# Row transposes placed between two projections, reordered queues and identity products in a fused attention and expert kernel

## The reference

```python
q = einsum('bse,hed->bhsd', x, Wq) + bq      # 16 heads of 64; k and v alike
scores = where(causal, q @ k.T / sqrt(64), -inf)
out = softmax(scores) @ v                    # heads joined: 1024 columns
x = layernorm(x + out @ Wo + bo)
xn = layernorm(x) * gamma + beta
probs = softmax((xn @ router_w.T) / 1.5)
w, idx = top_k(probs, 2)                     # 8 experts, 2 for each token
y = sum over the two experts of w * (silu(xn @ W1[e]) @ W2[e])
x = layernorm(y + x)
```

## Time and profile before

| | |
|---|---|
| Time, median of 3 runs | 1347.1 us (1345.36 to 1347.86) |
| Time of the profiled execution | 1345.8 us |
| Its span | 1344.0 us |
| PE busy | 1297.7 us, 97% |
| DVE busy | 1116.6 us, 83% |
| ACT busy | 1037.2 us, 77% |
| POOL busy | 491.7 us, 37% |
| Chain that ended last | PE 93%, ACT 2%, DVE 2% |

### The profile page before, as it was taken

How to read it: one execution, slowest core, us unless ns; L and a number is a source line. 1 busy time by engine, 2 the same in 40 slices (tenths; PEclk the granted TensorE clock), 3 DMA queues, 4 the chain that set the end, 5 groups by cost and what they waited for, 6 DMA issues and landing times.

```text
span 1344.0 us, 35085 instructions
## 1 busy us (share of the span) xinstructions
PE 1297.7 (97%) x10918; PEld 1134.5 (84%) x10918; DVE 1116.6 (83%) x5412; ACT 1037.2 (77%) x3402; POOL 491.7 (37%) x1067
## 2 busy tenths in 40 slices
PE   6999999999999999999999999999998999999967
PEld 5888888888888888888888888888887999999953
DVE  6888888888888888888888888888886898888847
ACT  7888888888888888888888888888884555555527
POOL 1023333333333333333333333333335665555545
PEclk9999999999999999999999999999999999999989
DMA  2000000000000000000000000000033777666638
GB/s 82 2 5 17 16 16 19 13 14 13 14 13 13 14 14 14 13 14 18 16 18 15 14 13 14 13 14 14 14 140 114 216 221 219 213 214 209 205 123 327
DMA packets 67641, 89.74 MB, mean 67 GB/s; under 512 B 10352, under 2 KB 37107, under 8 KB 67456
## 3 DMA queue, kind: packets, MB, share of 16 engines
q1 hardware_dynamic: 57808, 70.28, 16.6%
q0 software_dynamic: 8640, 17.13, 3.8%
q10 hardware_dynamic: 1008, 0.08, 0.1%
HBM read 61.66 MB, written 26.71 MB: 66 GB/s over the span
## 4 chain that ended last, share of the span: by engine, by line
PE 93%; ACT 2%; DVE 2%; issue 1%; DMA 1%; POOL 0%; ACTq 0%; POOLq 0%; SPq 0%; DVEq 0%
PE ps_f L1036 15%; PE ps_b L1070 14%; PE ps_a L1036 13%; PE ps_s L1077 12%; PE ps_s L1058 10%; PE ps_s L1235 9%; PE ps_b L1244 5%; PE ps_a L1244 5%; PE ps_s L1061 4%; PE ps_s L1311 2%; PE ps_a L1226 1%; ACT probs L574 1%; PE ps_f L1102 1%; PE ps_s L1082 1%; ACT probs L576 1%
## 5 line engine op out<-in xcount | busy, mean ns | idle before, releaser
L574 ACT ACTIVATE probs<-probs,neg_max 128x256 f32<-128x256 f32 x512 | 255.3, 499 | 127.8 <-DVE neg_max L790 125.4
L786 DVE CUSTOM_DVE_ANT_0 probs<-ps_s,mask 128x256 f32<-128x256 f32 x512 | 214.4, 419 | 37.1 <-PE ps_s L1061 34.3
L450 POOL TENSOR_SCALAR ln_b<-mv 128x2 f32<-128x2 f32 x32 | 6.1, 190 | 637.4 <-DVE mv L853 637.4
L1070 PE MATMUL ps_b<-pt,f_y 128*64 128x256 f32 (+1 forms) x2048 | 196.0, 333 | 10.3 <-ACT f_y L569 7.3
L660 ACT ACTIVATE m_tanh<-ps_s 128x256 f32<-128x256 f32 x284 | 108.8, 384 | 124.7 <-PE ps_s L1235 114.8
L1077 PE MATMUL ps_s<-ident,probs 128*128 128x128 f32 x1536 | 204.7, 274 | 0.0
L576 ACT ACTIVATE probs<-probs,neg_max 128x128 f32<-128x128 f32 x512 | 198.7, 388 | 0.0
L800 DVE TENSOR_SCALAR probs<-probs,inv_sums 128x256 f32<-128x256 f32 x512 | 180.8, 353 | 9.1
L1070 PEld LDWEIGHTS ps_b<-pt,f_y 128*64 128x64 f32 x2048 | 132.0, 137 | 61.0 <-issue 16.3
L540 POOL DMA_INDIRECT y_tok<-m_y,m_dest x142 | 139.7, 984 | 111.5 <-DVE m_dest L946 79.4
L1058 PE MATMUL ps_s<-qk 64*128 64x256 f32 x1024 | 171.3, 408 | 7.9 <-ACT pt L605 1.7
(11 more groups left out here) (193 smaller groups left out, 2988.5 us busy)
## 6 DMA issues: line engine op xcount, KB each, us to landing
m_w<-in_w SPq DMA_DIRECT2D x142, 256.0 KB
m_x<-queue SPq DMA_DIRECT2D x71, 133.0 KB, 3.0
f_y<-y_tok SPq DMA_DIRECT2D x32, 256.0 KB, 6.5
queue<-empty SPq DMA_DIRECT2D x8, 532.0 KB, 5.0
x_raw<-in_x SPq DMA_DIRECT2D x32, 128.0 KB, 2.1
out_x<-f_y SPq DMA_DIRECT2D x16, 256.0 KB, 5.7
y_tok<-m_y,m_dest POOLq DMA_INDIRECT x142
queue<-z,slot_now POOLq DMA_INDIRECT x128, 2.4
```

Source lines behind the costliest of these rows:

```text
L574: act.activation(row[:, 0:2 * P], row[:, 0:2 * P], ACT.Exp, scale=-1.0, bias=neg_max[:, pair, h, 0:1], accum_out=sums[:, d % 2, pair, h, 0:1])
L786: dve.tensor_tensor_reduce(out=row[:, 0:2 * P], in0=ps_s[:, pair, h, 0:2 * P], in1=mask[:].rearrange("p a b -> p (a b)"), scale=-1.0, scal ...
L1070: ins = pe.matmul(ps_b[r, cols], v[:, k, c * P + h * DH:c * P + (h + 1) * DH], pt[:, pair, h, src], start=(k == 0), stop=(k == 1), skip_gr ...
```

## The change

Seven edits:

1. *Rows between the projections.* In step q == 3 TensorE transposes `z` between the q and k projections of pair 0 and pair 1, into the banks of pair 1, behind waits for `z_done` and for the last maxima; it waits for `xnt_done` ahead of the transposes of pair 1. ScalarE does the `xnt` scaling ahead of both `evacuate_qk` and `first_pt`. The scores of pair 0 no longer wait for `xnt_done`.
2. *Start.* ScalarE rounds the second half of the weights behind the first two `evacuate_qk`. VectorE makes their rests in step 0 (two) and step 1 (one).
3. *Table.* Parts 3 to 6 do what 4 to 7 did, one step earlier.
4. *Step 127.* VectorE does `second_pt` ahead of `normalise(d, 1)`.
5. *Last expert steps.* `rows(68)` moves from j = 70 to j = 69, behind `rows(67)`; `rows(69)` goes ahead of `keep(70)`.
6. *Ranks.* `ranks(SEQS)` goes behind `output(0)` at j = 1.
7. *Identity products.* TensorE multiplies `ident` by `ident`, six times behind the first transposes and 42 times behind `output(NJ - 1)`. Nothing reads the results.

```diff
@@ -579 @@ scalar
-            for half in range(2):
+            def round_weights(half, i):
                 cols = slice(half * 512, (half + 1) * 512)
...
+            for i in range(3):
+                round_weights(0, i)
             act.wait_ge(small_loaded, 16 * 7)
             act.wait_ge(biases_ready, 1)
             evacuate_qk(0, 0)
             evacuate_qk(0, 1)
+            for i in range(3):
+                round_weights(1, i)
@@ -620 @@ scalar, step
+                if q == 3 and n in MID:
+                    act.wait_ge(zt_ready, n)
+                    act.activation(xnt[:].rearrange("p (i t) -> p i t", i=TILES), ps_s[:, 1, :, 3 * P:4 * P],
+                                   ACT.Identity, scale=gamma_sb[:, 0:1], bias=beta_sb[:, 0:1]).then_inc(xnt_done, 1)
                 if d >= 2 and q == 0:
                     copy_outputs(d)
                 if d + 1 < LAST:
                     evacuate_qk(d + 1, 0)
-                if q == 3 and n in MID:
-                    act.wait_ge(zt_ready, n)
                 if 1 <= d <= LAST:
                     first_pt(d)
-                if q == 3 and n in MID:
-                    act.activation(xnt[:].rearrange("p (i t) -> p i t", i=TILES), ps_s[:, 0, :, 3 * P:4 * P],
-                                   ACT.Identity, scale=gamma_sb[:, 0:1], bias=beta_sb[:, 0:1]).then_inc(xnt_done, 1)
@@ -700 @@ vector
             rest_of_weights(0, 2)
-            for i in range(3):
-                rest_of_weights(1, i)
@@ -739 @@ vector, first_table (likewise parts 5, 6, 7 become 4, 5, 6)
+                if part == 3:
+                    past_experts(0, NJ1)
                 if part == 4:
-                    past_experts(0, NJ1)
+                    count_experts(0, NJ1)
...
@@ -896 @@ vector, step
-                if n == SEQS - 1 and q == 3:
-                    first_table(7)
...
+                if d == 0:
+                    rest_of_weights(1, 0)
+                    rest_of_weights(1, 1)
+                if d == 1:
+                    rest_of_weights(1, 2)
                 if q == (3 if n < SEQS - 1 else 1):
                     evacuate_first_v(n * 4 + 3, 1)
+                if d == LAST - 1:
+                    second_pt(d)
                 if d < LAST:
                     normalise(d, 1)
-                if d >= 1:
+                if 1 <= d < LAST - 1:
                     second_pt(d)
@@ -988 @@ vector, experts
-                if j >= 2:
+                if 2 <= j < NJ - 1:
                     rows(j - 2)
+                if j >= NJ - 2:
+                    rows(j - 1)
                 keep(j)
...
-            rows(NJ - 2)
             rows(NJ - 1)
@@ -1159 @@ tensor, step
-                        if pair == 0 and q == 0 and n >= 2:
-                            pe.wait_ge(xnt_done, n - 1)
...
-                    for pair in range(2):
-                        qk_projection((d + 1) // QUADS % 2, (d + 1) % QUADS * 2 + pair, pair)
+                    qk_projection((d + 1) // QUADS % 2, (d + 1) % QUADS * 2, 0)
+                if q == 3 and n in MID:
+                    pe.wait_ge(z_done, n)
+                    pe.wait_ge(max_done, d * 4 + 4)
+                    for i in range(TILES):
+                        ins = pe.transpose(ps_s[:, 1, i, 3 * P:4 * P], z[:, (n - 1) % 2, i, 0:D], ident[:])
+                    ins.then_inc(zt_ready, 1)
+                if d + 1 < LAST:
+                    qk_projection((d + 1) // QUADS % 2, (d + 1) % QUADS * 2 + 1, 1)
                 if 1 <= d <= LAST:
                     pe.wait_ge(probs_done, d * 2 - 1)
                     pe.wait_ge(max_done, min(d * 4 + 2, LAST * 4))
                     transpose_probs((d - 1) % 2, 0).then_inc(pt_first_ready, 1)
-                if q == 3 and n in MID:
-                    pe.wait_ge(z_done, n)
-                    for i in range(TILES):
-                        ins = pe.transpose(ps_s[:, 0, i, 3 * P:4 * P], z[:, (n - 1) % 2, i, 0:D], ident[:])
-                    ins.then_inc(zt_ready, 1)
                 if 1 <= d <= LAST:
                     pe.wait_ge(max_done, min(d * 4 + 4, LAST * 4))
+                if q == 3 and n in MID:
+                    pe.wait_ge(xnt_done, n)
@@ -1211 @@ tensor
+            def keep_clock(dst, count):
+                for i in range(count):
+                    pe.matmul(dst, ident[:], ident[:], start=True, stop=True)
+
             transpose_input(0)
+            keep_clock(ps_b[:, 0:P], 6)
@@ -1280 @@ tensor, experts
-                if j == 1:
-                    pe.wait_ge(r_diff_done, SEQS - 1)
-                    pe.wait_ge(chosen_any_done, SEQS - 1)
-                    pe.wait_ge(res_done, SEQS * TILES)
-                    ranks(SEQS)
...
                 if j >= 1:
                     output(j - 1)
+                if j == 1:
+                    pe.wait_ge(r_diff_done, SEQS - 1)
+                    pe.wait_ge(chosen_any_done, SEQS - 1)
+                    pe.wait_ge(res_done, SEQS * TILES)
+                    ranks(SEQS)
             output(NJ - 1)

+            keep_clock(ps_s[:, 0, 0, 0:P], 42)
```

More of the change, by code:

```diff
@@ L581, in _ @@
             act.activation(xt_hi[:, 0, :], ps_f[:, 0:S], ACT.Copy).then_inc(xt_hi_done, 1)
-            for half in range(2):
+            def round_weights(half, i):
                 cols = slice(half * 512, (half + 1) * 512)
-                for i in range(3):
-                    act.wait_ge(attn_w_loaded[half * 3 + i], 16)
-                    act.activation(wqkv_hi[:, i, cols], wqkv_raw[:, i, cols], ACT.Copy, scale=SCALE if i == 0 else 1.0
-                                   ).then_inc(attn_w_hi, 1)
+                act.wait_ge(attn_w_loaded[half * 3 + i], 16)
+                act.activation(wqkv_hi[:, i, cols], wqkv_raw[:, i, cols], ACT.Copy, scale=SCALE if i == 0 else 1.0
+                               ).then_inc(attn_w_hi, 1)
+            for i in range(3):
+                round_weights(0, i)
             act.wait_ge(small_loaded, 16 * 7)
@@ L741, in first_table @@
                     link(dve.tensor_scalar(t_jump[:], t_steps[:], -float(ROWS), float(CAP), ALU.mult, ALU.add))
+                if part == 3:
+                    past_experts(0, NJ1)
                 if part == 4:
-                    past_experts(0, NJ1)
+                    count_experts(0, NJ1)
                 if part == 5:
-                    count_experts(0, NJ1)
-                if part == 6:
                     find_offsets(0, NJ1)
@@ L749, in first_table @@
                                                   in1=t_offset[:, 0:NJ1], op0=ALU.mult, op1=ALU.add))
-                if part == 7:
+                if part == 6:
                     dve.tensor_scalar(tab_w[:, 0:NJ1], t_expert[0:1, 0:NJ1], float(E - 1), float(HID), ALU.min, ALU.mult)
```

## The result

| | before | after |
|---|---|---|
| median of the executions, us | 1346.68 (1345.36 to 1347.86) | 1329.51 (1328.79 to 1331.43) |
| ratio | | 0.9875, 95% interval 0.9858 to 0.9892 |
| profiled execution: time, span | 1345.8, 1344.0 | 1331.43, 1329.6 |

The kernel became 17.2 us faster, where 12.7 were forecast; 1329.5 lies in the range of 1328.0 to 1341.5, near its low end.

What follows compares the result with a forecast made beforehand. TensorE, busy 97% of the span, was taken to bound the kernel. The terms -9.9 - 0.1 + 0.4 - 0.8 - 1.2 - 1.1 = -12.7 us took 1347.1 to 1334.4 us; range 1328 to 1341.5.

Steps and rivals of the forecast that it cites:

- The passages: Step q == 3 to next q == 0: rows between projections remove ScalarE's break, 0.33 us in 30 passages, -9.9 us.
- Table, step 127, last passage: Sequence 31: earlier table parts and second_pt ahead of normalise, -0.1 us at the attention output, bounds -1.0 and +0.5.
- Start: Kernel start: reordered roundings and rests, VectorE's cost not fully covered, +0.4 us; six identity products win nothing.
- Ranks: Expert stage: ranks behind output(0) are ready before VectorE asks, -0.8 us, bounds 0 to -0.9.
- Last writes: End of the expert stage: GpSimd goes on without its break, last write 1.16 us earlier, counted as -1.2 us.
- The estimate of 0.3 to 0.6 given back: Last GpSimd writes: VectorE locking GpSimd out could give back 0.3 to 0.6 of the 1.2 us; not included.
- Identity products at the end: Pause before the final stage: 42 products, 9.4 us, keep the clock up, -1.1 us, range 0 to -2.4.
- Profiled execution and median: Whole kernel: profiled execution would give 1333.1 us; the median, 1.3 us above it, was forecast at 1334.4.
- The pause did not stay: Rival at the passages: a new wait takes back the gain, only the ends' -2.8 us remains, 1344.3; chance 0.11.
- neither overran nor lost the clock: Case of clock or overrun; chance 0.12. If the clock falls at the end anyway, that gain is 0.
- `z` was late: Slower rival: z late at all 30 passages, +38 us, 1382; decides from z about 1.0 us later; chance 0.05.
- the whole pause goes: Case at the passages: the pauses vanish whole, bound 30 x 0.45 us; chance 0.08.

Runs made afterwards that it cites:

- r1_rows_only: Kernel before with only the rows moved between the projections and xnt moved ahead of the copies; 1334.34 against 1346.95 us, ratio 0.9902.
- r2_no_rows: Changed kernel with the row edit taken back and all other edits kept; 1341.5 us, ratio 0.9953 to the kernel before.
- r5_after_again: Changed kernel measured once more, nothing altered; 1329.72 against 1347.85 us for the kernel before, ratio 0.9871.
- r12_filled_start_old: Kernel of r9_filled_again with the start order as before the change, identity products kept; 1329.41 us.
- r9_filled_again: Changed kernel with identity products in three more TensorE pauses, second measurement, on another chip; 1329.49 against 1346.02 us for the kernel before.
- r7_z_later_3: Changed kernel with three more unread powers of 128x2 on GpSimd ahead of z; 1384.14 us, ratio 1.0274 to the kernel before.
- r11_filled_writes_old: Kernel of r9_filled_again with the last rows of the expert stage written in the old order; 1329.93 us.
- r6_z_later_1: Changed kernel with one more unread power of 128x2 on GpSimd ahead of z; 1343.5 us, ratio 0.9971 to the kernel before.
- r3: Changed kernel with the old start order and without the six identity products; 1330.75 us, ratio 0.9872 to the kernel before.
- r4_no_end: Changed kernel without the 42 identity products at the end; 1332.0 us, ratio 0.9886 to the kernel before.

## Why the prediction was right, and where it was not

The direction, the main term and the mechanism held; the gain was 4.5 us larger than the sum. Term by term, from the profiled execution of before to that of after (14.4 us), each with what the experiments make of it:

**The passages, -9.9.** They gave 30 x 0.366 = -11.0. The order of ScalarE came out as worked out, nearly to the hundredth: `first_pt` was forecast 1.90 behind the rows' new place and v 3.79, and they start 1.90 and 3.78 behind it (412.60 and 414.48, from 410.70). v still ends last: the attention output starts 0.25 behind its end in the passages of both kernels. Of the 0.04 that the forecast lacked, half is v's start and half v's own length (0.60 for 0.62, medians of 29 passages). The profile lists no idle time on TensorE there, because the modelled end of the scores hides it, but from the scores to the attention output it is still 1.61, 0.10 more than in rows 4. (The three passages with a margin of 0.95 for `z` don't stand in the trace: 29 of the 30 have 0.51 to 0.57, sequence 30 has 0.3. Nothing hangs on them.) r1_rows_only and r2_no_rows show that this edit, and no other, changes the interval.

**Table, step 127, last passage, -0.1.** It gave -1.7 (L, with the place of the rows and one interval's gain taken out: -0.74 - 1.36 + 0.37). 1.3 of it is the half clock at the attention output, which the text had named and left in the range, as I could not tell whether it would come again. The table shortens the steps of sequence 31 ahead of the rows by some 0.6 (r1_rows_only has the last rows 33.82 after the 30th, the changed kernel 33.23), where 0.3 was forecast. Some 0.2 was lost again, with the late `z` now ahead of both groups of transposes; no run separates it. The 0.6 are in the main a wait that went: in the kernel before, the second scores of step 127 waited for `next_slot`, which VectorE did behind part 6 of the table, in step 126.

```profile
1011.03 0.70 PE L1058 MATMUL ps_s<-qk 64*128 64x256 f32 x4 [0.73 <-DVE next_slot L881]
```

The changed kernel has no wait there. No run has the table's edit alone. The statement that `second_pt` wins little behind the new place of the rows was right (0.04), and r2_no_rows shows that with the rows in the old place it would have won 0.98.

**Start, +0.4.** In the profiled execution +0.96 (-0.40, and 1.36 for the place). All of it is the half clock in step 1, which was not foreseen: r5_after_again, without it, is 0.99 quicker from the bias to the row transposes. The order itself costs nothing: r12_filled_start_old shows the forecast loss of 0.4 behind the first scores, and a gain of 0.5 ahead of them, so the term was sized 0.4 to 0.5 too high. The six identity products at the start were called worth nothing, because the bias is ready only after 10.47. That premise was thin: in the same trace the projections end at 10.7 (9.58 in the changed kernel). In other executions the bias comes earlier, and in r9_filled_again `evacuate_qk` starts at 9.56 behind the projections and not behind the bias, so there quicker projections count. No run undid the six products alone with the new order; what they are worth stays open.

**Ranks, -0.8.** -0.85 or -0.86 in every kernel that has the edit (X 266.87 to 266.01), but -0.48 in r7_z_later_3.

**Last writes, -1.2.** The last write came 1.14 to 1.16 earlier, as worked out. At the end of the kernel the medians show 0.44 of it (r11_filled_writes_old), with spreads of 1.4 and 2.3 us; how much arrives is not settled. The estimate of 0.3 to 0.6 given back rested on the Trainium skill's rule on VectorE and GpSimd (SBUF — State Buffer, Who interferes with whom), a lockout; line 540 shows none at this place (980 to 1012 ns before, 0.98 at the end after). An interference of the two engines does show in this kernel: r6_z_later_1 has it at `z`, 1.15 for 0.88, beside `normalise`. The rule names this form, a tensor_scalar from and to SBUF; the 0.13 by which each `z` instruction grew is less than the length of the instructions beside it.

**Identity products at the end, -1.1.** -0.72 in the profiled execution, 0.4 to 1.1 by F of the pairs with and without, 0.5 by the medians on one chip. The duration (9.54 for 9.4), the fill of the pause and the clock were right. The second sum decides, as forecast: VectorE waited 1.68 for it. TensorE could load its weights 8.95 after the last write (8.77 in rows 12), and VectorE had it 2.02 later, where 1.8 was counted; together these are the 0.4 that is missing.

**Profiled execution and median.** The sum was made against an execution 1.3 us below its median and carried over with that distance. After, the profiled execution stands 1.9 above its median. Of this 3.2 us the two profiled executions of the changed kernel explain 1.85: 0.97 for half a clock in step 1 and 0.88 for the landing of the bias's input. These 3.2 us are the largest part of the miss of 4.5, and no term of the sum. The passages add 1.1 and the last passage 1.6, of which 1.3 is the clock; start and end take off 0.9, and another 0.4 goes off because the median of the kernel before is 1346.7 here and not 1347.1. That 1329.5 still lies in the range is in part luck: its bounds were made from the terms and say nothing of this distance between executions.

**The rivals.** The pause did not stay (r1_rows_only would have been near 1344), the 42 products neither overran nor lost the clock, and `z` was late only in the last passage. The case "the whole pause goes" (about 1330, with a chance of 0.08) has the number that came nearest, but not the mechanism: v was still last in the passages, which gave 0.366 each, nearer to the 0.33 of the forecast than to the 0.45 of this case.

What was not tried: the wait for the rows moved behind `first_pt` and nothing else; there TensorE would write the rows into a bank while `first_pt` reads it. So which share of the 0.366 is the wait's alone and which the earlier `xnt`'s stays open. Open too is why the loads of the final stage reach TensorE 3.4 to 4.9 us after their start from one kernel to the next.

## What to carry to other kernels

Where a wait of 0.2 us comes back once a sequence, look for what is queued behind the waiting instruction on its engine, and move the producer into a place where its input is ready and its consumer isn't; then say how late the producer may be, since beyond that room the same edit costs its full delay each time (here 0.5 us of room, a gain of 0.37, and 54 us lost at 2.2 us of delay). A gain at one mark is not yet a gain at the end: an order that brings the first scores 0.5 us forward lost the same behind them, and of 1.15 us at the last write the medians show 0.4. Before a term of 1 us is argued over, compare two profiled executions of one kernel, as they can differ by nearly 2 us in the start alone.

## What the runs showed of the hardware

- TensorE's granted clock fell to 0.5 (1.2 GHz) at two places: in the start in one of the two traces of the changed kernel, in the last passage in before, r3, r4, r6 and r7 and not in the others. In the start it had waited 1.8 to 1.9 us just before; in the last passage it had waited 1.17, 0.76 and 1.42 with short work between them (r4_no_end), or 3.0 in one piece (rows 5). In five traces with these waits filled with identity products it fell at neither place. The fall costs 1.0 to 1.1 us in the start and 1.3 to 1.6 in the last passage.
- GpSimd's tensor_scalar of 128x128 took 0.58 instead of 0.45 us where VectorE's tensor_scalar instructions of 0.35 and 0.28 us ran beside it from its start (r6_z_later_1), and VectorE's own were little longer (0.32 and 0.39 for 0.28). Where such an instruction began 0.30 after GpSimd's (the changed kernel), GpSimd's kept its 0.45.
- A load whose issue waits for scattered writes began 2.29 to 2.30 us after the last of them started on GpSimd, in each of the fourteen traces.
